# Rounded feed-forward stage: turned products copied with a lag of two tiles, and squares summed in other steps

## The reference

```python
def _act_quant(x):
    scale = 127.0 / jnp.clip(jnp.max(jnp.abs(x), axis=-1, keepdims=True), 1e-05)
    xq = jnp.clip(jnp.round(x * scale), -128.0, 127.0) / scale
...
gate = jax.nn.silu(_bitlinear(x, w_gate))          # 128 -> 512
up = _bitlinear(x, w_up)                           # 128 -> 512
return _bitlinear(gate * up, w_down)               # 512 -> 128
```

## Time and profile before

| | us |
|---|---|
| median of 3 runs | 2842.12 |
| lowest, highest | 2833.24, 2864.39 |
| profiled execution | 2834.13 |
| its span on the core | 2832.3 |
| rounded stage, first to last instruction | 2034.3 to 2120.9 |
| recurrent stage, delta rule's first to last step | 1262.0 to 1999.8 |

### The profile page before, as it was taken

The page is one execution under the profiler, slowest core; times in us unless marked ns, Lnnn a source line. Parts: engine busy times, 40 slices in busy tenths (PEclk is TensorE's granted clock), DMA queues, the critical chain, the costliest instruction groups (busy, mean ns, idle before and its releaser), DMA issues. The chain is left out here.

```text
span 2832.3 us, 91584 instructions
## 1 busy us (share of the span) xinstructions
PE 2407.7 (85%) x36874; PEld 1708.9 (60%) x36874; DVE 1648.4 (58%) x7006; ACT 1103.0 (39%) x4214; POOL 751.4 (27%) x1223
## 2 busy tenths in 40 slices
PE   5998878786399899779999999999658878999998
PEld 3555666665255456556666767665425556777774
DVE  3543555555545354357777777775345855667674
ACT  1332333332123343235555656564354423333332
POOL 1210000000122000127676767676243300000000
PEclk9997555555589999899999999999659955999998
DMA  2000000000100000125454545354100000000000
GB/s 97 3 3 2 2 2 2 3 2 2 40 2 3 2 1 0 70 54 116 104 116 101 118 100 121 96 121 109 45 1 1 2 2 2 2 3 3 2 3 15
DMA packets 110107, 104.24 MB, mean 37 GB/s; under 512 B 90496, under 2 KB 90496, under 8 KB 108800
## 3 DMA queue, kind: packets, MB, share of 16 engines
q1 hardware_dynamic: 109696, 98.50, 14.0%
HBM read 90.08 MB, written 8.39 MB: 35 GB/s over the span
## 5 line engine op out<-in xcount | busy, mean ns | idle before, releaser
L671 POOL TENSOR_TENSOR l2r_beta_s<-l2r_state,l2r_beta_f 128x256 f32<-128x256 f32 x512 | 370.0, 744 | 195.8 <-ACT l2r_state L574 194.6
L827 DVE TENSOR_TENSOR l2r_pre<-l2r_o_ps,l2r_beta_s 128x256 f32<-128x256 f32 x512 | 197.4, 419 | 85.7 <-PE l2r_o_ps L454 77.2
L574 ACT ACTIVATE l2r_state<-l2r_pre 128x256 f32<-128x256 f32 x512 | 190.0, 417 | 50.8 <-DVE l2r_pre L827 50.0
L140 PE MATMUL l0r_bank<-main_x,l0r_wx_half 128*128 128x32 f32 (+2 forms) x480 | 147.2, 406 | 60.7 <-ACT l0r_out_gate L196 60.1
L140 PEld LDWEIGHTS l0r_bank<-main_x,l0r_wx_half 128*128 128x128 f32 x480 | 116.0, 303 | 81.9 <-ACT l0r_out_gate L196 79.7
L1824 PEld LDWEIGHTS l3r_bank<-main_x,l3r_wx_half 128*128 128x128 f32 x480 | 95.6, 225 | 90.0 <-issue 44.8
L442 PE MATMUL l2r_d_ps<-l2r_state,l2r_kq 128*32 128x128 f32 x2056 | 148.0, 280 | 0.9 <-ACT l2r_state L574 0.7
L194 ACT ACTIVATE l0r_gates<-l0r_bank 128x24 f32<-128x24 f32 x256 | 48.6, 190 | 234.3 <-PE l0r_bank L152 234.3
L1963 ACT ACTIVATE l3r_gates<-l3r_bank 128x24 f32<-128x24 f32 x256 | 48.6, 190 | 222.8 <-PE l3r_bank L1836 222.8
L454 PE MATMUL l2r_o_ps<-l2r_rows,l2r_outer 32*128 32x128 f32 x2048 | 129.8, 323 | 4.6 <-DVE l2r_rows L819 1.3
L1807 POOL TENSOR_SCALAR main_y<-l3r_h_ring 128x128 f32<-128x128 f32 x16 | 8.4, 528 | 472.0 <-DVE l3r_h_ring L2117 472.0
(11 more groups left out here) (591 smaller groups left out, 7015.6 us busy)
## 6 DMA issues: line engine op xcount, KB each, us to landing
l2r_beta_f<-l2r_beta_store SPq DMA_DIRECT2D x256, 256.0 KB, 3.3
main_odd_layers<-in_l SPq DMA_DIRECT2D x1, 4826.5 KB, 14.6
main_odd_layers<-in_l SPq DMA_DIRECT2D x1, 3928.0 KB, 16.9
l2r_v_store<-l2r_v_part SPq DMA_DIRECT2D x32, 96.0 KB, 5.8
l2r_v_rows<-l2r_v_store SPq DMA_DIRECT2D x16, 192.0 KB, 4.6
main_decay<-in_decay SPq DMA_DIRECT2D x1, 3072.0 KB, 10.0
main_even_layers<-in_l SPq DMA_DIRECT2D x1, 2762.5 KB, 9.2
l2r_beta_store<-l2r_beta_tok SPq DMA_DIRECT2D x128, 16.0 KB, 1.6
```

The costliest lines, as they stand in the source:

```text
L140: nc.tensor.matmul(into, wx_half[:, g * P:(g + 1) * P], x_b[:, :, w * LW + lo:w * LW + hi].rearrange("p b t -> p t b"), start=False, stop= ...
L574: nc.scalar.activation(state[:, h * 2 * P:(h + 1) * 2 * P], pre[:, h * 2 * P:(h + 1) * 2 * P], ACT.Tanh).then_inc(state_ready[h], 1)
L671: nc.gpsimd.tensor_tensor(beta_s[:, half].rearrange("p (g r) -> p g r", g=HG), state[:, half].rearrange("p (g r) -> p g r", g=HG), beta_f[ ...
L827: nc.vector.tensor_tensor(pre[:, half].rearrange("p (c n) -> p c n", c=2), o_ps[:, 2 * h:2 * h + 2, 0:P], beta_s[:, half].rearrange("p (c ...
```

## The change

Nothing is computed otherwise; three things change.

1. In l2f, `copy_prod`, `down`, `scale_output` and `turn_output` run two tiles behind instead of one, and each engine has another order. Body n is now: TensorE `gate_and_up(n+1)`, (`turn_input`), `down(n-2)`, `turn_output(n-2)`, (`turn_integers`), `turn_prod(n-1)`; ScalarE `copy_prod(n-2)`, `gate(n+1)`, `scale_output(n-2)`, `scale_prod(n)`, (four `scale_input`), (`copy_integers`); VectorE `product(n)`, (`measure_input`), `add_output(n-2)`; GpSimd `round_prod(n)`, (`round_input`). The pieces of a group (in brackets) come in bodies with n % 4 == 0, and the integers' in those with n % 4 == 2. No buffer and no wait is added.
2. In l2f, one Silu on a 128x1 tile (`table_in`) is issued as soon as `magic` is there, ahead of the first `scale_input`.
3. In l2r, `SQ_STEPS` becomes (0, 1, 2, 3, 5, 6, 8, 9): the fifth sum moves from step 4 to 5, the seventh from step 7 to 8.

```diff
--- before.py
+++ after.py
@@ -253,7 +253,7 @@
 QUARTER, BETA_SLOTS = 4, 3
 OUT_PIECES = 8
 TCH = TC // 2
-SQ_STEPS = (0, 1, 2, 3, 4, 6, 7, 9)
+SQ_STEPS = (0, 1, 2, 3, 5, 6, 8, 9)
 WIDE = 7 * B
 UNREAD = {(True, False): 2, (True, True): 1, (False, True): 4, (False, False): 0}
 
@@ -2449,7 +2449,7 @@
         ones = mem.sb("ones", [P, P])
         wnum = mem.sb("wnum", [P, 3, BIT_INNER])
         wq = mem.sb("wq", [P, 3, BIT_INNER], BF16)
-        magic = mem.sb("magic", [P, 1])
+        magic, table_in = mem.sb("magic", [P, 1]), mem.sb("table_in", [P, 1])
         top, quant, back = mem.sb("top", [P, NT]), mem.sb("quant", [P, NT]), mem.sb("back", [P, 2, NT])
         top_p, quant_p, back_p = (mem.sb(n, [P, NT]) for n in ("top_p", "quant_p", "back_p"))
         num, yq = mem.sb("num", [P, GROUP, P]), mem.sb("yq", [P, GROUP, P], BF16)
@@ -2489,7 +2489,7 @@
                 round_input(0)
                 for n in range(NT):
                     round_prod(n)
-                    if n % GROUP == 1 and n // GROUP + 1 < NG:
+                    if n % GROUP == 0 and n // GROUP + 1 < NG:
                         round_input(n // GROUP + 1)
 
             @block.tensor
@@ -2547,19 +2547,18 @@
                 turn_integers(0)
                 pe.wait_ge(s["wq_ready"], 1)
                 gate_and_up(0)
-                for n in range(NT + 1):
-                    if n >= 1:
-                        turn_prod(n - 1)
-                    if n % GROUP == 3 and n + 1 < NT:
-                        turn_integers(n // GROUP + 1)
+                for n in range(NT + 2):
                     if n + 1 < NT:
                         gate_and_up(n + 1)
-                    if n >= 1:
-                        down(n - 1)
                     if n % GROUP == 0 and n // GROUP + 1 < NG:
                         turn_input(n // GROUP + 1)
-                    if n >= 1:
-                        turn_output(n - 1)
+                    if n >= 2:
+                        down(n - 2)
+                        turn_output(n - 2)
+                    if n % GROUP == 2 and n // GROUP + 1 < NG:
+                        turn_integers(n // GROUP + 1)
+                    if 1 <= n <= NT:
+                        turn_prod(n - 1)
 
             @block.scalar
             def _(act):
@@ -2604,24 +2603,25 @@
                     nc.scalar.activation(out[:, n % 2, :], out_ps[:, 0:P], ACT.Identity, scale=back_p[:, n:n + 1]).then_inc(s["out_ready"], 1)
 
                 act.wait_ge(s["magic_ready"], 1)
+                nc.scalar.activation(table_in[:, :], magic[:, :], ACT.Silu)
                 for n in range(GROUP):
                     scale_input(n)
                 copy_integers(0)
                 gate(0)
-                for n in range(NT + 1):
-                    if n >= 1:
-                        copy_prod(n - 1)
-                    if n % GROUP == 3 and n + 1 < NT:
-                        copy_integers(n // GROUP + 1)
+                for n in range(NT + 2):
+                    if n >= 2:
+                        copy_prod(n - 2)
+                    if n + 1 < NT:
+                        gate(n + 1)
+                    if n >= 2:
+                        scale_output(n - 2)
                     if n < NT:
                         scale_prod(n)
-                    if n + 1 < NT:
-                        gate(n + 1)
-                    if n >= 1:
-                        scale_output(n - 1)
-                    if n % GROUP == 1 and n // GROUP + 1 < NG:
+                    if n % GROUP == 0 and n // GROUP + 1 < NG:
                         for m in range(GROUP):
                             scale_input((n // GROUP + 1) * GROUP + m)
+                    if n % GROUP == 2 and n // GROUP + 1 < NG:
+                        copy_integers(n // GROUP + 1)
 
             @block.vector
             def _(dve):
@@ -2678,12 +2678,12 @@
                 dve.wait_ge(wchain, 6)
                 nc.vector.tensor_scalar(wq[:, :, :], wnum[:, :, :], -1.0, None, ALU.max).then_inc(s["wq_ready"], 1)
                 for n in range(NT + 2):
+                    if n < NT:
+                        product(n)
+                    if n % GROUP == 0 and n // GROUP + 1 < NG:
+                        measure_input(n // GROUP + 1)
                     if n >= 2:
                         add_output(n - 2)
-                    if n < NT:
-                        product(n)
-                    if n % GROUP == 1 and n // GROUP + 1 < NG:
-                        measure_input(n // GROUP + 1)
 
 
 def threshold_stage(nc, tag, x, dst, draws):
```

## The result

| us | before | after |
|---|---|---|
| median (runs) | 2841.68 (4) | 2804.50 (4) |
| lowest, highest | 2833.24, 2864.39 | 2800.21, 2810.40 |
| profiled execution, its span | 2834.1, 2832.3 | 2805.7, 2803.9 |
| l2f, first instruction to end of the last | 86.7 | 65.7 |
| l2f, GpSimd's first to last rounding | 67.17 | 46.39 |

The ratio is 0.9868, with a 95% interval of 0.9825 to 0.9911: 1.3% faster, and the interval reaches down to 0.9%. The kernel before was timed again beside the experiments: its medians there are 2835.0 us (14 runs), 2834.9 (11) and 2838.0 (7). Its four runs here stand higher, and 1.3% may be too much for that; against 2835.0 it would be 1.1%. Of the 28.4 us between the two profiled executions, l2f gives 21.0 and l2r's delta rule 8.2. Everything else together is 0.8 us longer, and single stages scatter by up to 2.4 us.

What follows compares the result with a forecast made beforehand. In l2f a chain through several engines, not one engine, was taken as the bound. Gains of 20.1 + 0.5 + 5.3 = 25.9 us brought the profiled 2834.1 to 2808.2; forecast 2812 us, range 2797 to 2828.

Steps and rivals of the forecast that it cites:

- the first case: The whole kernel: the sum of the three parts' gains, 25.9 us, holds as it stands; chance 50%.
- Part 1: The new order in l2f: first to last rounding takes 47.1 us against 67.2, a gain of 20.1 us.
- Loop A: l2f, one tile: turn_prod, copy_prod, down, scale_output, turn_output to the next turn_prod; 2.55 us.
- rival 1: l2f: TensorE's granted clock rises from 0.50, total gain 30 us, 2804 on the profiled execution; chance 20%.
- The bounds of 2.55 and 3.3: l2f, us per plain tile: lower is Loop A alone, upper the old loop less only the output's way; 2.65 taken.
- loop C: l2f, two tiles: product to scale_prod, copy, scale_output, addition, next product; 5.1 us, 2.6 a tile.
- Part 2: The early Silu in l2f: moves the 1.28 us table load, already partly hidden; gain 0 to 1.28, taken as 0.5 us.
- Part 3: The moved sums in l2r: 0.38 us in each of 13 bodies, 0.4 in k = 16, together 5.3 us.
- The place between profile and median: The whole kernel: 2812 us, put between profiled sum 2808.2 and 2816.2, which keeps the median's 8 us distance.
- Rival 2: l2f: VectorE's small operations wait for GpSimd's roundings, about 0.5 us a tile, 8 us; gain 18, 2816 us; chance 12%.
- Rival 3: l2r: the moved sums give nothing or cost a little; total gain 17 to 21, about 2815 us; chance 15%.
- Rival 4: l2r: moved sums land whole on the path in steps 5 and 8, costing 1.76 us a body, 22.9; 2836 us; chance 3%.

Runs made afterwards that it cites:

- e1: The kernel before with only the new l2f order and the early Silu, SQ_STEPS left as before: 2813.96 us, ratio 0.9928.
- e13: The kernel before, unchanged, profiled a second time: delta rule 735.28 us, its late body 47.1 us.
- e11: The changed kernel with only VectorE's order undone, add_output(n-2) again ahead of product(n): 2840.7 us in one run.
- e14: Repeat of the changed kernel with one sum put back from step 5 to step 4: 2831.5 us, where the first run took 2808.9.
- e2: The kernel before with only SQ_STEPS changed, l2f as before: 2830.13 us, ratio 0.9978.
- e3: The kernel before with only VectorE's order changed, product(n) ahead of add_output(n-2), run once: l2f stage 81.2 us.

## Why the prediction was right, and where it was off

It said 2812 us (2797 to 2828), by the first case; 2804.5 was measured.

**Part 1** held. The sum gave 47.1 us from first to last rounding, and 46.39 was measured. Loop A was put at 2.55 and took 2.66 us, because TensorE goes on 0.27 and not 0.20 us behind the turned output, and the copy follows at 0.67. The tile was put at 2.65; the 0.10 meant for waits between the loops happened to cover this error, and that is luck. A group of four took 13.14 for 13.35, with 3.4 us of it at the upper clock. I estimate that the clock gave 1.1 us up to the last rounding (see rival 1), so without it 47.5 us would stand beside 47.1. The bounds of 2.55 and 3.3 held. One sign did not come: VectorE's product was never to wait for an addition, and it does so in the timeline above, by loop C, which was put at 5.1 us and is estimated at 5.16. The tail is the same chain where the last tile took 2.66 us (e1: 5.17 us from the last rounding's start, before 5.14). In the changed kernel's profile the last rounding came 2.30 us behind the one before it, after the upper clock, the last turned product then stood behind an older tile's output on TensorE, and the tail took 5.50: the 0.36 us was given back. l2f gave 21.0 us for 20.6 predicted with part 2.

**Part 2**: 0.55 measured, 0.5 predicted.

**Part 3** had the right mechanism and one term a little off. The gain of step 4 (0.50 for 0.51) and of steps 7 and 8 together (0.36 for 0.35) stood as worked out. What steps 5 and 6 give back is 0.42 (0.13 and 0.29), not 0.48, so a body gained 0.44, not 0.38. Against e13, which like the changed kernel kept its clock in l2r, the 13 bodies gave 5.7 us and k = 16 another 0.4, 6.0 for 5.3. The other 2.2 of the profile's 8.2 us are nearly all the fallen clock in the late body of the kernel before. That was in its trace when I predicted. I had read one ordinary body and taken it for all of them. A fall of the clock was no term of the sum, nor a rival in this stage.

**The place between profile and median** was a choice, and the wrong way: 2812 stood 4 us above the profiled sum of 2808.2. The profiled execution came to 2805.7. The runs of the changed kernel spread over 10 us, where before's spread over 31. The sum's 0.91% lay just short of the prediction's 1% and the measured 1.3% just over it: the likeliest case came true, on the side to which I had given 38%. This is the term that moved the outcome most, and it is spread of the runs more than work removed; the four runs of the kernel before had their median 7 us above the 2835.0 of its 14 later ones. The spread goes with the granted clock of the whole run: of the eleven runs of the kernel before beside e11 to e14, the two longest (2863.6 and 2856.7 us) have 0.829 and 0.830, the nine others (2830.2 to 2841.1 us) 0.837 to 0.843.

**Rival 1** (the clock rises, 30 us) was true for 10 of 65 us only. In the last of its three stretches two tiles, from the rounding at 2081.32 to the one at 2086.28, took 4.96 us for 5.32. From these I estimate what it gave: 0.36 in each stretch, 1.1 us. Its time of 2804 is the measured median, but it did not come by its mechanism. **Rival 2** is refuted: L2653 starts at 2079.92, inside a rounding that runs from 2078.66 to 2080.58, and takes 0.15 us as in the earlier trace rows; no VectorE operation of the chain grew. The Trainium skill ("SBUF — State Buffer", "SBUF: two separate sides") names such a lock for certain forms; these rows show none. **Rival 3** is refuted by e2 (728.72 us for the 735.28 of e13, which had no fall of the clock in l2r either). **Rival 4** is refuted by the steps: 5 and 6 grew by 0.42 together, 8 got shorter.

## What to carry over

Where no engine is the bound, write the loops down from start to start and take the longest: loop A's 2.55 us came within 0.11 of the measured tile. Write down those that are nearly as long as well, since a cure that opens only the longest gains only the distance to the next, and keep the clock apart when two tiles are compared. In doing so follow the queues, not the data: e11's loop ran over two tiles by the data and over one by ScalarE's queue, and the same lag that gains 15 us behind VectorE's new order loses 15 without it. A piece moved to the next step of a serial chain is worth only what the receiving step does not give back, and a stage of many equal bodies has to be read through once for the one that is not equal.

## What the runs showed of the hardware

The granted clock of TensorE fell by itself in the middle of a long stage in some runs of a program and not in others, 0.4 to 1.9 us after the end of the same wait of 1.45 us before the same instruction, for 3.4 to 64.9 us. Each such time cost about a third of its length (6.8 us: 49.3 for 47.1; 64.9 us: 753.7 for 730.6 in the whole delta rule, with TensorE at 66.0 us busy out of 66). That longest fall cost 23.1 us, and the profiled executions of the kernel before and the changed one differ by 28.4. So a single pair of times would not do here. e14's rows:

```profile
1784.00:1850.00 66.00, 66.00 (x778) 48.13 (x775) 33.47 (x151) 26.05 (x120) 31.94 (x57) 0.51 0.30 75
1850.00:1900.00 50.00, 47.36 (x873) 34.82 (x871) 38.62 (x175) 28.90 (x134) 36.30 (x69) 1.00 0.46 106
```

In e14, TensorE works without a gap for 66 us at the lower level (1.2 GHz) before the clock returns. In the same stage of e3 it returned after 3.4 us.
